# Conditioning of a token-routed layer: new engine programs, gate sigmoids read from PSUM, a recurrence in three parts, rows turned through one bank

## Time and profile before

| | us |
|---|---|
| median of 3 runs | 1209.62 (1207.29 to 1212.23) |
| profiled execution, its own time | 1209.29 |
| its span, first to last instruction | 1207.6 |
| busy in the span: PE / DVE / ACT / POOL | 1044.7 / 664.6 / 530.4 / 320.0 |
| mean granted TensorE clock | 0.947 of full |

### The profile page before, as it was taken

One profiled execution on the slowest core, in us unless ns is written; L12 is line 12 of the kernel. 1 busy time (PEld: TensorE's weight loads), 2 busy tenths in 40 slices (PEclk: granted clock), 3 DMA queues, 4 the chain that ended last, 5 costly groups with the idle time before them and its releaser, 6 DMA issues.

```text
span 1207.6 us, 16920 instructions
## 1 busy us (share of the span) xinstructions
PE 1044.7 (87%) x5022; PEld 823.6 (68%) x5023; DVE 664.6 (55%) x942; ACT 530.4 (44%) x848; POOL 320.0 (26%) x248
## 2 busy tenths in 40 slices
PE   2367896794997539999999999999999999999994
PEld 1233453352444439998999899989898888999883
DVE  5885996995987323334333433355555344343553
ACT  5738456546554313334333333344545334333553
POOL 4774653682780530002000200020201102000202
PEclk9999898997998559999999999999999999999998
DMA  4980020120220261115312611283536234211711
GB/s 150 318 254 0 1 105 0 45 96 1 85 91 1 106 211 70 69 69 139 87 69 69 157 69 69 78 218 124 152 137 200 70 139 135 81 69 69 218 70 21
DMA packets 62878, 124.25 MB, mean 103 GB/s; under 512 B 4710, under 2 KB 4746, under 8 KB 62856
## 3 DMA queue, kind: packets, MB, share of 16 engines
q1 hardware_dynamic: 54200, 106.86, 25.3%
q0 software_dynamic: 8656, 17.13, 7.0%
HBM read 91.99 MB, written 35.22 MB: 105 GB/s over the span
## 4 chain that ended last, share of the span: by engine, by line
PE 59%; issue 1%; ACT 1%; DVEq 1%; DVE 1%; POOL 0%; ACTq 0%; POOLq 0%
PE ps_y L1350 10%; PE ps_y L1351 10%; PE ps_y L1352 10%; PE ps_h L1330 10%; PE ps_h L1332 9%; PE ps_h L1331 9%; PE ps_t L1300 1%; POOL out_dram L1279 0%; ACT xh L1445 0%; ACT y L1452 0%; DVEq L1390 0%; DVE hl L1507 0%; ACT w1h L1417 0%; DVE w1l L1468 0%; ACTq L1390 0%
## 5 line engine op out<-in xcount | busy, mean ns | idle before, releaser
L1330 PE MATMUL ps_h<-xh,w1h 128*128 128x320 f32 (+3 forms) x768 | 247.6, 322 | 8.1 <-issue 3.8
L1332 PE MATMUL ps_h<-xh,w1l 128*128 128x320 f32 (+3 forms) x768 | 243.7, 317 | 0.0
L1331 PE MATMUL ps_h<-xl,w1h 128*128 128x320 f32 (+3 forms) x768 | 243.6, 317 | 0.0
L1279 POOL DMA_INDIRECT out_dram<-y,token x40 | 64.8, 1619 | 658.0 <-ACT y L1452 488.5
L1507 DVE SCALAR_TENSOR_TENSOR hl<-ps_h,hh 128x320 fp32r<-128x320 f32 (+1 forms) x192 | 106.9, 558 | 193.0 <-ACT hh L1441 184.3
L1350 PE MATMUL ps_y<-w2h,hh 128*128 128x512 f32 x528 | 206.5, 391 | 1.7 <-DVE hl L1507 1.6
L1351 PE MATMUL ps_y<-w2h,hl 128*128 128x512 f32 x528 | 206.7, 392 | 0.0
L1352 PE MATMUL ps_y<-w2l,hh 128*128 128x512 f32 x528 | 206.1, 390 | 0.0
L1471 DVE TENSOR_TENSOR w2l<-raw,w2h 128x512 fp32r<-128x512 f32 x128 | 88.6, 692 | 196.9 <-ACT w2h L1420 194.0
L1441 ACT ACTIVATE hh<-ps_h 128x320 fp32r<-128x320 f32 (+1 forms) x192 | 94.2, 491 | 230.9 <-PE ps_h L1332 228.2
L426 PE MATMUL ps_mm<-ratios,wm 128*128 128x512 f32 x384 | 175.3, 612 | 20.6 <-DVE ratios L999 12.0
(11 more groups left out here) (180 smaller groups left out, 1204.1 us busy)
## 6 DMA issues: line engine op xcount, KB each, us to landing
raw<-in_L_ffn_w_dram SPq DMA_DIRECT2D x64, 1024.0 KB
slots<-r_rows SPq DMA_DIRECT2D x8, 1302.5 KB, 15.5
rows<-slots SPq DMA_DIRECT2D x8, 1302.5 KB
f_rows<-in_fside_BxSxS_dram SPq DMA_DIRECT2D x4, 1024.0 KB, 6.5
rows<-in_x_dram SPq DMA_DIRECT2D x4, 1024.0 KB, 6.4
out_dram<-rows SPq DMA_DIRECT2D x4, 1024.0 KB, 4.7
slots<-r_rows POOLq DMA_DIRECT2D x1, 1302.5 KB
rows<-slots SPq DMA_DIRECT2D x5, 260.5 KB, 3.8
```

What stands on the lines that cost most here:

```text
L1330: nc.tensor.matmul(o, w1h[:, j, dt, :], xh[:, dt, lo:hi], start=(dt == 0), stop=False)
L1331: nc.tensor.matmul(o, w1h[:, j, dt, :], xl[:, dt, lo:hi], start=False, stop=False)
L1332: last = nc.tensor.matmul(o, w1l[:, j, dt, :], xh[:, dt, lo:hi], start=False, stop=(dt == CT - 1))
```

## The change

The four kinds of edits, all in `conditioning_and_routing`:

- `IN_PSUM` is 4: `gate_sum` copies tiles 0 to 7 only. `gate_functions` becomes `gate_inputs` (Silu, Sigmoid of z_dec) and `gate_sigmoid(k)` for k = 8 to 11, each from its PSUM bank.
- `recurrence` becomes `decay_inputs`, `states` and `products_y`; `fold` keeps the scans, `complete` is its second half; on POOL `products` loses its first half to `ek_products`, and `newton` its numerator add to `own_add`. Semaphores are split to match.
- rows of x2 and r2 are turned through ps_to alone in batches 0 to 2 (in batch 3 through ps_to and ps_f, and r2 through ps_mm and ps_x).
- every engine's list of calls has a new order.

```diff
-IN_PSUM = 2
+IN_PSUM = 4
...
-    row_bank = lambda i: (ps_to, ps_x)[i % 2]
+    x2_bank = lambda b, i: ps_to[:] if b < B - 1 or i % 2 == 0 else ps_f[:]
+    r2_bank = lambda b, i: ps_to[:] if b < B - 1 else ps_x[:] if i == 3 else ps_mm[:, i, :]
...
         clear_slots(NE // 2, NE + 1)
+        sp.wait_ge(s_f_tp, 3 * CT)
+        load_f(3)
         store(0)
         sp.wait_ge(s_x2_out, 16)
         load_x(2)
-        sp.wait_ge(s_f_tp, 3 * CT)
-        load_f(3)
...
+        def own_add(u):
+            r = u % 2
+            pool.wait_ge(s_num, 2 * u + 2)
+            pool.wait_ge(s_eukv, u + 1)
+            for i in range(2):
+                last = g.tensor_tensor(sums[r][:, i, 0], sums[r][:, i, 0], eukv[:, r, i], ALU.add)
+            last.then_inc(s_own, 1)
...
                 if b >= 2:
-                    pe.wait_ge(s_ev_r2, TT * (b - 1))
+                    pe.wait_ge(s_x2, CT * (b - 2) + 2)
...
-            if k >= 3:
+            if 3 <= k < 11:
                 pe.wait_ge(s_z, Z_COPIES * b + k - 2)
+            if k == 11:
+                pe.wait_ge(s_gates, CT * b + 1)
...
                     if dt == 0 and e == 0:
-                        pe.wait_ge(s_z, Z_COPIES * (b + 1))
+                        pe.wait_ge(s_gates, CT * b + 2)
...
                     if dt == 0 and e == 2:
-                        pe.wait_ge(s_gates, CT * (b + 1))
+                        pe.wait_ge(s_gates, CT * b + 3)
+                    if dt == 0 and e == 3:
+                        pe.wait_ge(s_gates, CT * b + 4)
...
-        def gate_functions(b):
-            act.wait_ge(s_z, Z_COPIES * b + 2 * CT)
+        def gate_inputs(b):
+            act.wait_ge(s_z, Z_COPIES * b + CT)
             a.activation(z_in[:], z_in[:], ACT.Silu)
+            act.wait_ge(s_z, Z_COPIES * (b + 1))
             a.activation(z_dec[:], z_dec[:], ACT.Sigmoid).then_inc(s_dec, 1)
...
+        def gate_sigmoid(b, k):
+            z, bias, e = gate_source(k)
+            act.wait_ge(s_mm, 12 * b + k + 1)
+            a.activation(z[:, e], ps_mm[:, k % 3, :], ACT.Sigmoid, bias=bias).then_inc(s_gates, 1)
...
-        def recurrence(b):
-            steps = Steps(dve, s_rec_steps, REC_STEPS * b)
+        def decay_inputs(b):
             dve.wait_ge(s_dec, b + 1)
...
+        def states(b):
+            dve.wait_ge(s_rec_steps, REC_STEPS * b + 1)
...
+        def products_y(b):
```

More of the change, by code:

```diff
@@ L846, in _ @@
         first_reciprocal(10)
+        first_sums(11)
         gate_sum(2, 6)
[L848 removed]
+        x2_row(1, 2)
+        x2_row(1, 3)
         gate_sum(2, 7)
[L850 removed]
+        gate_inputs(2)
+        gate_sigmoid(2, 8)
+        gate_sigmoid(2, 9)
+        gate_sigmoid(2, 10)
+        copy_x(3, 0)
+        r2_row(1, 0)
+        gate_sigmoid(2, 11)
+        exponentials()
+        first_reciprocal(11)
+        copy_x(3, 1)
+        own(12)
         r2_row(1, 1)
[L852 removed]
+        copy_x(3, 2)
@@ L890, in _ @@
-        gate_sum(3, 7)
-        gate_sum(3, 8)
-        gate_sum(3, 9)
-        first_reciprocal(14)
-        first_sums(15)
-        gate_functions(3)
-        exponentials()
-        for i in range(TT):
-            r2_row(2, i)
+        own(14)
+        gate_sum(3, 5)
+        own(15)
+        gate_sum(3, 6)
+        first_sums(14)
+        gate_sum(3, 7)
+        gate_inputs(3)
+        first_sums(15)
+        gate_sigmoid(3, 8)
+        gate_sigmoid(3, 9)
+        gate_sigmoid(3, 10)
+        gate_sigmoid(3, 11)
@@ L1151, in _ @@
         backward(15)
-        recurrence(3)
+        fold(14)
         fold(15)
+        decay_inputs(3)
+        states(3)
+        products_y(3)
+        complete(14)
+        complete(15)
         select(2, routing[2])
+        residual(3)
+        place(2, routing[2])
         ratio(14)
-        place(2, routing[2])
-        residual(3)
         ratio(15)
```

564 lines of the change are left out of this document (323 added, 241 removed).

## The result

The changed kernel is faster. Its median is 1180.38 us in 4 runs (1176.28 to 1182.25); the kernel before, run beside it on the same chip, stands at 1210.14. The forecast was 1174 with a range of 1160 to 1196, so sign and range held, and the gain is 30 us where 35 were expected. The profiled execution is the fastest of the four: 1176.28 us of its own time, span 1174.6.

A forecast was written before the change was run, and what follows sets the result against it. No engine was full in the first 445 us; the order in which engines meet each other's results set the length. Gains reaching -36.8 us at batch 3's logits, plus 1.7, gave -35: from 1209.62 to 1174 us, range 1160 to 1196.

The forecast's parts named there:

- Gates: Silu behind gate_sum 7: 6.4 us on ACT covered by PE's gates 8 to 10; z_gate waits under 2 us.
- Recurrence: DVE's recurrence in three parts adds no work; 2.29 + 4.57 us lie under gates 9 to 11, only products remain.
- Rows through one bank: Rows each wait for ACT to empty the bank; 1.80 us bare, costed at nothing where gates stand between.
- The start: ACT and DVE at the front: Ln later, first scan 26.2 against 18.17, gates 0 at 77.2 against 70.04, +7.
- Station D: Start of gates 3 on PE: 292.0 against 319.62, -27.6, with a 12.9 us ACT chain ahead of the projection.
- the price of a collision: DVE steps contended by POOL on the path: one POOL add, about 1.2 us, charged for each.
- C's terms: Start of gates 2 on PE: gates, logits, rows, projection, places and place(0) summed to 220.0 against 226.72, -6.7.
- Station E: Logits of batch 3 on PE: 371.2 against 408.03, -36.8, including DVE's 10.44 us wait for POOL gone.
- The +1.7 us that the sum adds outside the stations: A handful of semaphore steps and one more cold start, worth +1.7 us, bringing -36.8 to -35.
- Rival 3: DVE 90% full in 28 to 408 us's work; excess of about 32 us grows by half, +16: 1190; chance 0.18.

The follow-up runs named there:

- The run with POOL's wait: Changed kernel with one GpSimd wait added: own_add(10) waits for DVE's second output of batch 1; 1175.85 us, ratio 0.9736.
- the variant with the old POOL order: Kernel before with only the gate moves (four gate tiles in PSUM, early Silu, recurrence in parts ahead of place(1)); 1194.02 us, ratio 0.9856.
- placement later: Changed kernel with DVE's placement of batch 0 moved behind the residual of batch 1; 1179.39 us, ratio 0.9745.
- three moves: Changed kernel with batch 0's placement behind batch 1's residual, batch 1's second output ahead of fold 10, and the start reordered; 1171.76 us, ratio 0.9677.
- and dispatch later: The three moves kernel with the second half of dispatch 0 also behind newton(10) on POOL; 1169.26 us, ratio 0.9687.
- wait, moves: Changed kernel with POOL's own_add(10) waiting for batch 1's second output, batch 0's placement behind batch 1's residual, and the start reordered; 1175.42 us, ratio 0.9708.
- the variant with the dispatch later: Changed kernel with only the second half of dispatch 0 moved behind newton(10) on POOL; 1181.91 us, ratio 0.9739.

## Why the prediction was right, and where it was off

- **Gates: right, for the reason given.** The z_gate waits fell from 9.08, 10.76 and 14.42 to 0.20, 2.50 (over the 2 us that I had named as the bound) and none, and Silu started ahead of gate 10's sigmoid in each batch (111.63 against 118.52 in batch 0). "Without that cover the recurrence is as late as now" was too mild: without it the new kernel is 42 us slower, and slower than the old.
- **Recurrence: the place was right, "it adds no work" not quite.** DVE's scans of the state (L1092, both inputs in SBUF) rose from 1205 to 1452 ns in the mean, 4 us in all. What I had said of scans, that they never lengthen, was of those with the decay in PSUM, and it held (1.19 to 1.28 us in all profiles); the others had no price.
- **Rows through one bank: right.** The four waits that it makes, 2.9 us, lie beside the products y. The trace shows it; the run with two banks left them untouched and shows nothing of them.
- **The start: right in size, partly wrong in cause.** First scan at 24.49 (forecast 26.2, before 18.17), gates 0 at 78.57 (77.2). But putting the Ln back early, with the first reciprocal and sums ahead of the copy, gave some 3 us of the 8.5. In the changed kernel ACT stands 6.66 us at the copy of x 1, which waits for its load, with the first reciprocal behind it; with that undone too, its timeline still shows the copy waiting 5.02 us for the load of x 1, and gates 0 behind it. I had named this instruction and put no price on it.
- **Station D: the step that was off.** "I charged one POOL add (about 1.2) for each contended step on the path." For D the chain was written over ACT and PE (72.0); DVE's own chain was not walked through. Walked, it was the longer one: from the residual of batch 1 to that of batch 2, 220.0 to 297.6 us, DVE stands once, for 2.8 us, and two instructions on it, 9.92 for 2.35 and 6.71 for 2.47, have 11.8 us of excess (16.2 with all the others). The run with POOL's wait gives 3.8 us back of the 5.6 missed; where the other 1.8 belong stays open. The term of the sum that was mis-sized is the price of a collision: 1.2 us was taken for each, and a single one measured 7.6 here and up to 8.9 in a variant. Two slips of the adding are small beside it: C's terms give 218.9 and not 220.0, D's 263.1 and not 263.4.
- **Station E: right to 2 us** (77.5 against 79.2). DVE's 10.44 us ahead of the last ratio are gone: 371.06 and 372.20 us, no wait. In the variant with the old POOL order they are still there, 10.44 to the digit. The +1.7 us that the sum adds outside the stations did not show: from the last logits to the end it is 798.7 us, before 799.6.
- **Rival 3, "DVE becomes the bound"**, is in part what the 4 to 6 us are: DVE is busy 337.29 of the 352 us between first scan and last logits, 96%, against 311.48 of 380 before. I gave it 0.18 and +16 us on the path. DVE's busy time did grow by 14.9, near that, but only about 5 lay on the path, and it did not grow where I had it. The own-term add (L979) and the products (L1012) fell by 8.6 and 2.1 us; the bound on the denominator rose by 10.3, the second output by 5.2, the state's scans by 3.9. Over the four lines that I named the sum is +1.0, and the sign that I named, means of L979 and L993 above 2 us, did not come (1.42 and 1.57). It was not a case beside the forecast but a correction to it.
- **Profile against median.** The forecast was made against one execution. The profiled one of the changed kernel gained 33.0 us (1209.29 to 1176.28), 2 less than the sum; the other three ran at 1179.6 to 1182.3, while the kernel before spreads 0.4%. The two values of the step to gates 2, 78.9 and 83.1, could make most of that, but the other three have no profile, and the variant with PE's places later took 1180.77 us with the step at 78.9. So part of the spread stays open, and the forecast came nearer to the profiled execution (2 us) than to the median (6) partly by which execution that was.

The line that grew most, the bound on the denominator, has one operand in SBUF beside its bound. Before and after, even units (count | busy us, mean ns | idle before):

```profile
L981 DVE TENSOR_SCALAR sums_even<-sums_even,den_min 128x512 f32<-128x512 f32 x16 | 13.0, 854 | 0.3
L1063 DVE TENSOR_SCALAR sums_even<-sums_even,den_min 128x512 f32<-128x512 f32 x16 | 16.7, 1086 | 0.3
```

The Trainium skill, SBUF — State Buffer, section Who interferes with whom, says that the engine that starts first keeps the shared pair for its whole instruction while the other blocks. In this trace that caps a wait at one POOL instruction, 1.3 us. The rows where both engines lengthen (POOL's 3.67 for 2.49, DVE's 1.48 for 1.2) agree; the 9.92 and 11.22 us don't, and with them the collision price that I took from the milder rows failed.

## What to carry to other kernels

When a change closes the waits of one engine, walk the chains of the others through the same stretch before adding up: an engine that was 82% busy had to be 96% busy, and the forecast's one bad step was the one where its chain was not written out. Where VectorE and GpSimd share work, place the VectorE instructions that read PSUM (here the scans) beside GpSimd's longest run and those whose data lie in SBUF alone outside it, above all where the run follows indirect stores; a wait on the engine with slack can be cheaper than the overlap it prevents. Parts of a schedule change are not additive: all of this change but the early Silu is a loss of some 14 us against the old kernel. And a list tuned on one profile is tuned on one execution: the same list met different collisions in different executions.

## What the runs showed of the hardware that was not expected

**A VectorE instruction can be held for GpSimd's whole run.** An instruction of DVE with its data operands in SBUF that met POOL's run behind indirect stores ended one own length after the run's last instruction, however long that was. Six cases:

| kernel | DVE instruction | took, alone | ended | POOL's run ended | difference |
|---|---|---|---|---|---|
| before | L979 | 8.97, 1.2 | 254.72 | 253.64 | 1.08 |
| changed | L1109 | 9.92, 2.35 | 254.16 | 252.01 | 2.15 |
| placement later | L1109 | 11.22, 2.35 | 255.32 | 253.17 | 2.15 |
| three moves | L1060 | 7.92, 1.2 | 256.35 | 255.27 | 1.08 |
| and dispatch later | L1075 | 6.26, 1.2 | 236.24 | 235.16 | 1.08 |
| wait, moves | L1076 | 6.26, 1.2 | 236.71 | 235.64 | 1.07 |

POOL's instructions in these runs keep the lengths they have alone (1.26 and 2.5 for two). Where POOL had come out of a wait for another engine instead, the two took turns and both lengthened (the changed kernel at 269.80, the variant with POOL's wait at 252.65).

All fourteen profiles bear this out, over conditioning and routing. In POOL's runs that go on from an indirect store without a pause, 19 instructions of DVE were held for the rest of the run, by 2.2 to 9.0 us; the one such run that met any and held none is in the variant with the dispatch later, where two of the state's scans took 1.22 and 2.22 us beside two adds. In runs that began behind a wait or a pause, 758 instructions of DVE without an operand in PSUM started with at least two of POOL's still to come, and none was lengthened by more than 1.2 us. Two SBUF inputs are not needed: in three of the 19 it was the bound on the denominator (L1063), 5.6 us for 0.5; DVE's row of a pair of them in the variant with two banks, 0.5 us for the first and 5.6 for the second:

```profile
246.01 6.05 DVE L1063 TENSOR_SCALAR sums_even<-sums_even,den_min 128x512 f32<-128x512 f32 x2
```

The variant with POOL's wait puts a pause of 4.48 us between the stores and the run, and none of DVE's instructions that the run then meets is held (the longest excess is 1.1 us). That is one experiment beside a regularity; why the stores matter, no run here shows.

**The small instructions pay the same price.** Of those of 8 to 32 elements, 0.17 to 0.19 us, the ones that don't read PSUM or reduce take 0.9 to 1.2 beside GpSimd's adds of 1.26: the price goes by the neighbour's length, not by their own.
